# Input LayerNorm: inverse root through ScalarE, first tile in halves, two more weight remainders on GpSimd

## What is computed

```
def _layernorm(x, axis=-1, eps=1e-05):
    m = jnp.mean(x, axis=axis, keepdims=True)
    v = jnp.var(x, axis=axis, keepdims=True)
    return (x - m) / jnp.sqrt(v + eps)
...
xn = _layernorm(x, axis=-1)
...
for r in range(weight.shape[0]):
    mask = (edge_type == r).astype(x.dtype)
    sums = jax.ops.segment_sum(msgs * mask[:, None], dst, num_segments=n)
    cnt = jax.ops.segment_sum(mask, dst, num_segments=n)
    mean = sums / jnp.maximum(cnt, 1.0)[:, None]
    out = out + mean @ weight[r]
```

## Time and profile before

| | us |
|---|---|
| three runs | 2207.68, 2210.69, 2210.82 |
| median | 2210.69 |
| the profiled execution's own time | 2209.28 |
| its span, from first to last instruction | 2207.4 |
| TensorE busy (matmul) | 2186.2 |
| ScalarE, VectorE, GpSimd busy | 437.1, 1191.1, 729.6 |

### The profile page before, as it was taken

The page is one execution under the profiler, slowest core; times in us unless marked ns, Lnnn a source line. Parts: engine busy times, 40 slices in busy tenths (PEclk is TensorE's granted clock), DMA queues, the critical chain, the costliest instruction groups (busy, mean ns, idle before and its releaser), DMA issues.

```text
span 2207.4 us, 25123 instructions
## 1 busy us (share of the span) xinstructions
PE 2186.2 (99%) x9858; PEld 1776.8 (80%) x9858; DVE 1191.1 (54%) x1676; ACT 437.1 (20%) x605; POOL 729.6 (33%) x599
## 2 busy tenths in 40 slices
PE   7999999999999999999999999999999999999998
PEld 5878888888888888888888888889988888888887
DVE  6522578736666566665765577653432367234233
ACT  3221111111111111100121200112321314121121
POOL 4203002055655556544645454521210453000000
PEclk9999999999999999999999999999999999999999
DMA  7443321447788988783968789853126885103102
GB/s 262 171 131 97 109 83 48 131 167 235 245 292 281 317 297 304 243 279 131 323 225 316 240 290 304 273 181 135 48 77 220 277 284 169 38 33 123 59 31 79
DMA packets 191152, 416.59 MB, mean 189 GB/s; under 512 B 33937, under 2 KB 44562, under 8 KB 191034
## 3 DMA queue, kind: packets, MB, share of 16 engines
q1 hardware_dynamic: 127834, 229.10, 30.6%
q0 software_dynamic: 63200, 185.89, 25.4%
HBM read 352.34 MB, written 103.66 MB: 207 GB/s over the span
## 4 chain that ended last, share of the span: by engine, by line
PE 98%; DVE 1%; ACT 0%; DMA 0%; issue 0%; DVEq 0%; ACTq 0%
PE acc L946 90%; PE acc L941 5%; PE tp L810 2%; PE agg L852 1%; PE tp L838 0%; PE misc L838 0%; DVE Wlo L1087 0%; DVE stats L1110 0%; DVE aTlo L1092 0%; DMA xr<-in_x 0%; DVE stats L1104 0%; DVE xnb L1118 0%; DVE stats L1102 0%; PE misc L852 0%; DVE stats L1103 0%
## 5 line engine op out<-in xcount | busy, mean ns | idle before, releaser
L946 PE MATMUL acc<-Whi,aThi 128*128 128x512 f32 (+1 forms) x2880 | 1142.0, 397 | 5.5 <-DVE aTlo L1092 5.5
L946 PE MATMUL acc<-Whi,aTlo 128*128 128x512 f32 (+1 forms) x2880 | 1136.0, 394 | 0.0
L946 PE MATMUL acc<-Wlo,aThi 128*128 128x512 f32 (+1 forms) x2880 | 1132.4, 393 | 0.0
L946 PEld LDWEIGHTS acc<-Whi,aThi 128*128 128x128 f32 (+1 forms) x2880 | 534.5, 186 | 135.4 <-DVE aTlo L1092 6.3
L946 PEld LDWEIGHTS acc<-Whi,aTlo 128*128 128x128 f32 (+1 forms) x2880 | 534.5, 186 | 134.2
L946 PEld LDWEIGHTS acc<-Wlo,aThi 128*128 128x128 f32 (+1 forms) x2880 | 535.7, 186 | 131.6
L1623 POOL DMA_INDIRECT ring<-y_d,edge x390 | 489.2, 1254 | 424.2 <-DVE U L1287 153.9
L1087 DVE TENSOR_TENSOR Wlo<-Wraw,Whi 128x1024 fp32r<-128x1024 f32 x150 | 184.0, 1229 | 315.5 <-ACT Whi L956 315.0
L968 ACT COPY res<-acc 128x512 f32<-128x512 f32 (+1 forms) x180 | 105.7, 587 | 846.2 <-PE acc L946 832.1
L1287 DVE SCALAR_TENSOR_TENSOR U<-ring,edge,U 128x1024 f32<-128x1024 f32 x180 | 230.2, 1279 | 23.9 <-DMA ring<-y_d,edge 23.6
L1287 DVE SCALAR_TENSOR_TENSOR odd<-ring,edge,odd 128x1024 f32<-128x1024 f32 x170 | 217.4, 1279 | 25.8 <-DMA ring<-y_d,edge 25.6
(11 more groups left out here) (161 smaller groups left out, 1054.5 us busy)
## 6 DMA issues: line engine op xcount, KB each, us to landing
y_d<-res SPq DMA_DIRECT2D x144, 256.0 KB
Wraw<-in_L_gnn_weight SPq DMA_DIRECT2D x64, 512.0 KB, 5.7
Wraw<-in_L_gnn_w_gate SPq DMA_DIRECT2D x16, 512.0 KB, 7.1
ring<-y_d,edge POOLq DMA_INDIRECT x390, 6.2
xr<-in_x SPq DMA_DIRECT2D x9, 512.0 KB, 4.1
xn_d<-xnb SPq DMA_DIRECT2D x9, 512.0 KB, 4.9
xs_d<-xr SPq DMA_DIRECT2D x9, 512.0 KB, 5.7
ur_d<-res SPq DMA_DIRECT2D x18, 256.0 KB
```

Of the source, the lines that this page charges most:

```text
L946: mm = nc.tensor.matmul(to, a[:, k, rows(i)], b[:, s % 2, k, :], start=start, stop=stop)
```

## The change

The input's inverse root is taken by ScalarE's square root of `v + eps` (`root_x`), a reciprocal on VectorE and one Newton step, where it was a shift, a constant and three Newton steps. The semaphores `ln_var` and `ln_root` tie the two engines. Tile 0 is normalized in two halves of 512 columns, turned in two halves, its high parts copied in two halves, its low parts made in two halves (`lo_first`); unit 0 begins with the first half and waits for the second ahead of slice 4. GpSimd makes the low parts of granules 5 and 7 as well as 2 and 3, ahead of `rows_sum(0)`; VectorE makes those of 0, 1, 4 and 6. VectorE's list begins `ln_x(0)`, `lo_w(0)`, `lo_first(0)`, `lo_w(1)`, `lo_first(1)`, `ln_x(1)`, `lo_w(4)`, `lo_w(6)`. In ScalarE's list `root_x(0)` stands first, `root_x(1)` behind granule 5, and `root_x(t)` of later tiles ahead of slice 1 of the unit in `LN_AT`, so behind the eviction of the unit before.

```
@@ -52,7 +52,7 @@
 
 U_AT = [0, 4096, 8192, 12288, 18432, 22528, 26624, 38912, 43008, 47104]
 U_SEMS, TH_SEMS = 6, 4
-POOL_LO = (2, 3)
+POOL_LO = (2, 3, 5, 7)
 
 
 
@@ -360,8 +360,8 @@
         x_in = [sem(f"x_in{i}") for i in range(XS)]
         xn_st = [sem(f"xn_st{i}") for i in range(XS)]
         xs_st = [sem(f"xs_st{i}") for i in range(XS)]
-        ln_done, xs_made, x_turned, x_hi, x_lo = (
-            sem(n) for n in ("ln_done", "xs_made", "x_turned", "x_hi", "x_lo"))
+        ln_var, ln_root, ln_done, xs_made, x_turned, x_hi, x_lo = (
+            sem(n) for n in ("ln_var", "ln_root", "ln_done", "xs_made", "x_turned", "x_hi", "x_lo"))
         edges_in, edges_made, tail_made, codes_st, samples_in = (
             sem(n) for n in ("edges_in", "edges_made", "tail_made", "codes_st", "samples_in"))
         place_const, run_made, runs_in = sem("place_const"), sem("run_made"), sem("runs_in")
@@ -439,6 +439,11 @@
             n = GRAN * (s + 1) + i // 2 - 1
             return range(n, n + 1) if s + 1 < STAGES and i in (2, 4, 6, 8) else range(0)
 
+
+        def with_halves(t):
+
+            return t + 2
+
         def x_tiles(i):
 
             return len(range(i, T, XS))
@@ -711,7 +716,7 @@
 
             def x_rows(t):
 
-                sp.wait_ge(ln_done, t + 1)
+                sp.wait_ge(ln_done, with_halves(t))
                 sp.dma_start(xn_d[rows(t), :], xnb[0:width(t), t % XS, :]).then_inc(xn_st[t % XS], 16)
                 sp.wait_ge(xs_made, t + 1)
                 sp.dma_start(xs_d[rows(t), :], xr[0:width(t), t % XS, :]).then_inc(xs_st[t % XS], 16)
@@ -811,9 +816,16 @@
                 return tr
 
             def turn_x(t):
-                pe.wait_ge(ln_done, t + 1)
-                if t:
-                    pe.wait_ge(x_lo, t)
+                if t == 0:
+                    for h in range(2):
+                        pe.wait_ge(ln_done, h + 1)
+                        for k in range(4 * h, 4 * h + 4):
+                            tr = nc.tensor.transpose(tp[:, h, (k % 4) * 128:(k % 4) * 128 + 128],
+                                                     xnb[:, 0, k * 128:(k + 1) * 128], ident[:, :])
+                        tr.then_inc(x_turned, 1)
+                    return
+                pe.wait_ge(ln_done, with_halves(t))
+                pe.wait_ge(x_lo, with_halves(t - 1))
                 turn_rows(lambda k: xnb[0:width(t), t % XS, k * 128:(k + 1) * 128], width(t)).then_inc(x_turned, 1)
 
             def any_bad():
@@ -924,13 +936,15 @@
                         if q >= 3:
                             wait_evicted(pe, q - 3)
                         if s == 0:
-                            pe.wait_ge(x_lo, i + 1)
+                            pe.wait_ge(x_lo, with_halves(i) if i else 1)
                         if (kind, h) == (O_, 0):
                             pe.wait_ge(o_lo, i + 1)
                         if (kind, h) == (C_, 0):
                             pe.wait_ge(u_lo, i + 1)
                         if (kind, h) == (I_, 0):
                             pe.wait_ge(x1_lo, i + 1)
+                    if q == 0 and k == 4:
+                        pe.wait_ge(x_lo, 2)
                     if i == 0 and k % 2 == 0:
                         wait_w_lo(pe, GRAN * s + k // 2)
                     if kind in STANDING:
@@ -1033,10 +1047,23 @@
                         nc.scalar.activation(x_big[0:EP, :], x_raw[0:EP, :].bitcast(F32), ACT.Copy,
                                              scale=x_inv[0:EP, 0:1]).then_inc(x_ghi, 1)
 
+            def root_x(t):
+
+                act.wait_ge(ln_var, t + 1)
+                w = width(t)
+                nc.scalar.activation(stats[0:w, 15:16], stats[0:w, 14:15], ACT.Sqrt).then_inc(ln_root, 1)
+
+            root_x(0)
             for n in range(3):
                 hi_w(n)
-            hi_turned(0, x_turned, 1, x_hi)
-            for n in range(3, 8):
+            for h in range(2):
+                act.wait_ge(x_turned, h + 1)
+                half_k = slice(4 * h, 4 * h + 4)
+                nc.scalar.copy(aThi[:, half_k, rows(0)], turned_rows(128)[:, half_k, :]).then_inc(x_hi, 1)
+            for n in range(3, 6):
+                hi_w(n)
+            root_x(1)
+            for n in range(6, 8):
                 hi_w(n)
             for q in range(UNITS + 1):
                 if q == place(Q_, 0, 0):
@@ -1052,8 +1079,10 @@
                         cell_tanh(q - 1)
                     if q == UNITS:
                         continue
+                    if k == 1 and q in LN_AT:
+                        root_x(LN_AT[q])
                     if k == 3 and q in TURN_AT:
-                        hi_turned(TURN_AT[q], x_turned, TURN_AT[q] + 1, x_hi)
+                        hi_turned(TURN_AT[q], x_turned, with_halves(TURN_AT[q]), x_hi)
                     if k == 3:
                         for n in split_beside(q):
                             hi_w(n)
@@ -1092,17 +1121,6 @@
                 nc.vector.tensor_tensor(aTlo[:, :, rows(t)], turned_rows(width(t)), aThi[:, :, rows(t)].bitcast(F32),
                                         ALU.subtract).then_inc(done, 1)
 
-            def inverse_sqrt(v, y, work):
-
-                chain(nc.vector.tensor_scalar(v, v, LN_EPS, None, ALU.add))
-                chain(nc.vector.tensor_scalar(y.bitcast(I32), v.bitcast(I32), 1, None, ALU.logical_shift_right))
-                chain(nc.vector.tensor_scalar(y.bitcast(I32), y.bitcast(I32), -1.0, float(0x5F3759DF),
-                                              ALU.mult, ALU.add))
-                for _ in range(3):
-                    chain(nc.vector.scalar_tensor_tensor(work, y, v, y, ALU.mult, ALU.mult))
-                    chain(nc.vector.tensor_scalar(work, work, -0.5, 1.5, ALU.mult, ALU.add))
-                    chain(nc.vector.tensor_tensor(y, y, work, ALU.mult))
-
             def ln_x(t):
                 w = width(t)
                 dve.wait_ge(x_in[t % XS], 16 * (t // XS + 1))
@@ -1110,13 +1128,20 @@
                     step.inc(nc.vector.bn_stats(stats[0:w, 6 * h:6 * h + 6], xr[0:w, t % XS, half(h)]))
                 step.wait(dve)
                 chain(nc.vector.bn_aggr(stats[0:w, 12:14], stats[0:w, 0:12]))
-                inverse_sqrt(stats[0:w, 13:14], stats[0:w, 14:15], stats[0:w, 0:1])
+                v, y, work = stats[0:w, 14:15], stats[0:w, 15:16], stats[0:w, 0:1]
+                nc.vector.tensor_scalar(v, stats[0:w, 13:14], LN_EPS, None, ALU.add).then_inc(ln_var, 1)
+                dve.wait_ge(ln_root, t + 1)
+                chain(nc.vector.reciprocal(y, y))
+                chain(nc.vector.scalar_tensor_tensor(work, y, v, y, ALU.mult, ALU.mult))
+                chain(nc.vector.tensor_scalar(work, work, -0.5, 1.5, ALU.mult, ALU.add))
+                chain(nc.vector.tensor_tensor(y, y, work, ALU.mult))
                 if t >= XS:
                     dve.wait_ge(xn_st[t % XS], 16 * (t // XS))
                     dve.wait_ge(xs_made, t - XS + 1)
-                    dve.wait_ge(x_turned, t - XS + 1)
-                nc.vector.tensor_scalar(xnb[0:w, t % XS, :], xr[0:w, t % XS, :], stats[0:w, 12:13], stats[0:w, 14:15],
-                                        ALU.subtract, ALU.mult).then_inc(ln_done, 1)
+                    dve.wait_ge(x_turned, with_halves(t - XS))
+                for part in ((half(0), half(1)) if t == 0 else (slice(0, D),)):
+                    nc.vector.tensor_scalar(xnb[0:w, t % XS, part], xr[0:w, t % XS, part], stats[0:w, 12:13], y,
+                                            ALU.subtract, ALU.mult).then_inc(ln_done, 1)
 
             def edge_order():
 
@@ -1487,13 +1512,22 @@
                 dve.wait_ge(f_in[n % 3], 16 * (n // 3 + 1))
                 nc.vector.tensor_tensor(a, a, fx[0:w, n % 3, :], ALU.add).then_inc(out_made, 1)
 
+            def lo_first(h):
+
+                dve.wait_ge(x_hi, h + 1)
+                half_k = slice(4 * h, 4 * h + 4)
+                nc.vector.tensor_tensor(aTlo[:, half_k, rows(0)], turned_rows(128)[:, half_k, :],
+                                        aThi[:, half_k, rows(0)].bitcast(F32), ALU.subtract).then_inc(x_lo, 1)
+
             ln_x(0)
             lo_w(0)
+            lo_first(0)
             lo_w(1)
-            lo_turned(0, x_hi, 1, x_lo)
+            lo_first(1)
             ln_x(1)
             for n in range(4, 8):
-                lo_w(n)
+                if n not in POOL_LO:
+                    lo_w(n)
             for q in range(UNITS + 1):
                 for k in range(K):
                     if q and k == 0:
@@ -1513,7 +1547,7 @@
                     if q == UNITS:
                         continue
                     if k == 4 and q in TURN_AT:
-                        lo_turned(TURN_AT[q], x_hi, TURN_AT[q] + 1, x_lo)
+                        lo_turned(TURN_AT[q], x_hi, with_halves(TURN_AT[q]), x_lo)
                     if k == 0 and q in LN_AT:
                         ln_x(LN_AT[q])
                     if q == 17 and k == 6:
```

(2 more changed lines are left out.)

## The result

The change made the kernel a little faster, by about what was forecast: 2205.49 us median (2205.10 to 2207.10, 16 runs) against 2209.70 (2207.68 to 2212.00, 16 runs). The ratio is 0.9983, with a 95% interval of 0.9976 to 0.9989, so 2.4 to 5.3 us less; the 0.2% (4.4 us) that I counted as no change lies inside it. The forecast was 2206.7, in the range 2203.5 to 2210.9. The profiled execution took 2205.51 us with a span of 2203.7, where the one before took 2209.28 with 2207.4: 3.8 and 3.7 us less. Of the 1.2 us between the forecast and the measured median, 1.0 lies in the kernel before, whose median is 2209.70 over 16 runs and was 2210.69 over the first three; the gain was forecast as 4.0 us and measured as 4.2.

The account below looks back on a forecast made before the run. TensorE bounds the kernel, through unit 2's start, set by VectorE's list, and the clock behind it. Gain 31.5 - 29.1 + 1.6 = 4.0 us, so 2210.7 - 4.0 = 2206.7 us; range 2203.5 to 2210.9.

Parts of the forecast that it names:

- The frame: Whole kernel: time is unit 2's start (31.48 us before) plus a fixed rest and a clock correction; 4.0 us gained.
- effective starts: TensorE's gapless part: unit 2's start plus the lower clock's cost behind it, 31.5 + 1.6 = 33.1 us before.
- Root: Input normalization: `v + eps` to normalizing takes 1.26 us instead of 2.47, 0.42 of it ScalarE's root; 1.21 saved per tile.
- Tile 0: First tile in halves: unit 0 starts at 11.74 us instead of 13.58, 1.8 earlier; that edit alone moves no later unit.
- `ln_x(1)`, remainders 4 and 6: VectorE's list: a product stands until granule 5 ends at 18.71, normalizing ends 19.94; two remainders instead of four, 2.3 us less.
- Order A: VectorE's `lo_w(4)` goes before GpSimd's granule 7: unit 2 at 29.1 us, 4.0 us gained, chance 0.44.
- order B: GpSimd's granule 7 goes before VectorE's `lo_w(4)`: unit 2 at 31.5 us, full clock, 1.6 us gained.
- What binds unit 2, and the clock: Ahead of unit 2: VectorE's list sets its start, 29.1 us; a 1.5 us gap instead of 3.1 leaves the clock high.
- B: Rival at the remainders: granules handed to GpSimd cost what they save; 1.6 us gained, 2209.1 us, chance 0.26.
- D: Rival, slower: `ln_x(4)` waits on `root_x(4)` behind the fourth eviction, first unit store and `rows_sum(1)`; 2215 us, chance 0.03.
- C: Rival at VectorE's list: almost no meeting with GpSimd, unit 2 at 25.9; 7.2 us less, 2203.5 us, chance 0.10.
- port theory: From the experiments: VectorE's two-SBUF-input instructions and GpSimd tensor-tensors take turns, so meetings made or removed decide an edit's worth.

Follow-up runs that it names:

- e1_root: The new root alone, in the kernel before: 2205.32 us, ratio 0.9980.
- e4_root_halves: The whole change with granules 5 and 7 left to VectorE: 2206.20 us, ratio 0.9987.
- e2_halves: Tile 0 in halves alone, with the old root and granules 5 and 7 on VectorE, against the kernel before: 2211.37 us, ratio 1.0007.
- e3_pool: Granules 5 and 7 on GpSimd alone, all else as in the kernel before: 2211.79 us, ratio 1.0010.
- e11_after_again: The whole change, unedited, timed again: 2205.54 us, ratio 0.9980.
- e5_after_late: The whole change with `ln_x(2)` moved behind `lo_turned(1)` and `ln_x(3)` one unit later: 2204.55 us, ratio 0.9980.
- e6_sum_later: e4_root_halves with `rows_sum(0)` moved behind GpSimd's edge codes, ahead of `rows_sum(1)`: 2204.63 us, ratio 0.9977.
- e9_gapless: e4_root_halves with `rows_sum(0)` in GpSimd's wait for the edge lists, `ln_x(2)` and `ln_x(3)` both at unit 2 behind `lo_turned(1)`: 2202.42 us, ratio 0.9968.
- e7: e6_sum_later with `ln_x(2)` behind `lo_turned(1)` and `ln_x(3)` one unit later: 2207.14 us, ratio 0.9988.
- e8: e1_root with `rows_sum(0)` behind the edge codes and `ln_x(2)` behind `lo_turned(1)`: 2206.62 us, ratio 0.9987.

## Why the prediction was right

**The frame.** The time moved with the start of unit 2 and the clock behind it. The effective starts, 33.1 and 29.4, differ by 3.7 us, the spans by 3.7; the forecast was 4.0, and the missing 0.3 are VectorE's list, 0.2 late, and the rest of unit 1 behind it.

**Root.** The round trip over ScalarE took 0.42 us (5.89 to 6.31) and the first half was normalized from 7.15 on; 7.11 was forecast. This part alone carries the result (e1_root): 4.2 us by the medians, as much as all three. The prediction did not say which part carries the gain. With the new root the halves cost unit 2 some 1.3 us (e4_root_halves against e1_root), and the granules give next to nothing; the forecast schedule had both detours in, so its number did not rest on them.

**Tile 0.** Unit 0 started at 11.90 (forecast 11.74). Granule 2's cast was the wall, and it was 0.19 us later in this execution. That `lo_w(1)` meets granule 2 (2.40 us) was forecast. Without the new root the halves gain nothing (e2_halves). The prediction said that this edit "moves no later unit"; through `lo_w(1)` it does, and its own schedule of `ln_x(1)`, started at 14.54, had that in.

**`ln_x(1)`, remainders 4 and 6.** The product stood until 18.81 (18.71), normalizing ended at 20.04 (19.94), `lo_w(6)` at 24.50 (24.36), the turned low part at 29.23 (29.0). Order A came, by 0.09 us; e3_pool shows order B. I had left open whether GpSimd gets in between two VectorE instructions: it does.

**What binds unit 2, and the clock.** VectorE's list does, as forecast: in e11_after_again a wait of 1.36 us ahead of unit 2 (forecast 1.5) and 29.20 (forecast 29.1) with the clock up behind it, and e5_after_late took that wall away. What I had not forecast is the fall inside unit 1 in the first trace: unit 1 took from 21.23 to 29.41 us, 8.2 for the 6.4 forecast. By my own schedule TensorE would wait 1.6 us ahead of unit 1 (19.5 to 21.1), and I put nothing for the clock behind that wait; it was 1.82 us in the first trace, and the clock fell. This cost nothing by luck: VectorE's list ended at 29.23, about when the slower unit 1 did. With e5's order the same fall would show in full, an estimate of 1.8 us (8.2 less 6.4).

**What I had not placed.** ScalarE stands at `root_x(2)` until 26.17, in front of the first eviction and of the turned tile 1. The high part came at 27.76, the low part was started at 28.02: 0.26 us to spare, which the prediction did not count. Timeline of the changed kernel:

```profile
26.17 0.20 ACT L1054 ACTIVATE stats<-stats 128x1 f32<-128x1 f32 x1 [6.20 <-DVE stats L1132]
...
26.74 1.02 ACT L974 CAST aThi<-tp 128x1024 fp32r<-128x1024 f32 x1
```

**Rivals.** B (handed-over granules cost what they save) was right in its mechanism for the kernel without the other parts, and e4_root_halves shows that they add little to these. D's mechanism did not decide here, as forecast (first unit store at 38.12, forecast 38.3; fourth eviction at 41.66, forecast about 42), but it did in e6_sum_later, and not where I had looked. I gave the fourth eviction 7 us of cover. The fifth, in front of the turned tile 3, has 3.3 in the changed kernel: it ends at 47.80, the tile's cast starts at 49.42, the low part ends at 51.70 and unit 6 starts at 53.41. Nor did I price stores that stand behind each other (4.7 and 6.2 us from issue to landing in e6). C forecast 7.2 us less for a front that waits for nothing; e9_gapless, which has such a front, is 7.3 us ahead of the kernel before. The chances of a slower end add up to 0.08, where the text has 0.07.

**What stays open.** By the front alone e1_root should be 1.0 to 1.2 us ahead of the whole change; it is 0.2 ahead by the medians (2205.32 against 2205.49 and 2205.54), and not at all when each is taken against the kernel before timed beside it. The trace shows 1.0 us of it at the second normalization in one execution. That this happens in most executions was not shown. Nor was it tried to settle what sets the clock's rises and falls; from the first matmul to the first rise it was 3.9 and 4.4 us in two executions of the whole change, 4.85 before and 5.3 in e9_gapless (11.49 to 16.77).

**A row read too widely.** From the product at 28.09, which took its 0.16 us inside a tensor-scalar of GpSimd's, the prediction took it that tensor-scalars hold nothing up. That product was issued 0.30 us behind the tensor-scalar's start. One that is issued sooner stands until 0.46 us behind it (last section). This changes no term of the sum.

## What to carry to other kernels

Before work is handed to GpSimd, lay the two engines' two-input instructions side by side in time: each meeting costs VectorE the rest of GpSimd's instruction, and a [128 x 1] product of 0.16 us can stand for 2. Row sums that nobody waits for belong into GpSimd's own waits, and not in front of VectorE's critical list. When one front gets shorter, look at once for what stands behind it in the in-order queues (an eviction behind a store, a root behind an eviction); three kernels here lost at unit 4 or 6 (e7, e8; e6) much of what they had won at unit 2.

## What the runs showed of the hardware

- GpSimd's tensor-tensor holds a VectorE product up to its own end: in e6_sum_later a product issued at 29.50 ended at 30.15, where GpSimd's of 29.26 ended (30.13). A cast does the same, and so does the start of a tensor-scalar. In e6_sum_later (its timeline) the product takes 0.28 us for 0.16 and ends with the cast, at 30.66 and 30.65; the normalizing instruction behind it takes 1.45 us for 0.81 beside a tensor-tensor:

```profile
30.20 0.45 POOL L1630 CAST tmp<-raw_edges 125x320 f32<-125x320 int32 x1
30.38 0.28 DVE L1137 TENSOR_TENSOR stats<-stats 128x1 f32<-128x1 f32 x1
30.70 1.45 DVE L1143 TENSOR_SCALAR xnb<-xr,stats 128x1024 f32<-128x1024 f32 x1
30.73 0.87 POOL L1631 TENSOR_TENSOR code<-code,tmp 125x320 f32<-125x320 f32 x1
```

  In e3_pool (its timeline) a product that is issued with a tensor-scalar of 1.01 us takes 0.45 us for 0.22 and ends 0.46 us behind that one's start:

```profile
29.77 1.01 POOL L1595 TENSOR_SCALAR tmp<-tmp 125x320 f32<-125x320 f32 x1
29.78 0.45 DVE L1102 SCALAR_TENSOR_TENSOR stats<-stats 128x1 f32<-128x1 f32 x1
```

  In e9_gapless one issued 0.15 us behind the start (27.48) ended at 27.94, again 0.46 us behind it. Issued later, a product is not held: at 28.09 before, and in the timeline of e7_sum_later_late, 0.72 us behind the start:

```profile
26.71 1.02 POOL L1627 TENSOR_SCALAR code<-code 125x320 f32<-125x320 f32 x1
...
27.43 0.16 DVE L1137 TENSOR_TENSOR stats<-stats 128x1 f32<-128x1 f32 x1
```

  The Trainium skill ("SBUF — State Buffer", "Who interferes with whom") says that a VectorE instruction with two SBUF inputs contends with a GpSimd instruction that reads SBUF. For tensor-tensors, casts and a tensor-scalar's first 0.46 us the traces agree; for the rest of a tensor-scalar they do not, and the measurement decides. The port theory as it was set up, with tensor-tensors alone, is too narrow.
- With both engines' lists full they alternated in these places: GpSimd in between two VectorE instructions (granule 7, issued at 20.05 in the whole change, took 3.38 us: 0.99 of waiting and 2.39 of work), VectorE in between two of GpSimd (`lo_w(6)` behind granule 7, while `rows_sum(0)`, issued at 23.38, took 3.37 us for 2.39).
- The length of a wait of TensorE did not decide alone whether the clock fell behind it. It fell 1.3 us behind the end of a wait of 1.82 us in the whole change (22.53) and behind one of 2.27 us in e3_pool (25.12); it stayed up behind 1.45 us (e11_after_again), 1.71 (e4_root_halves), 2.3 (e2_halves, unit 1) and 2.45 us (e8_root_sum_later). So a wait of some 2 us left the clock alone in one execution and cost it in another; what decides was not settled.
